# Cross-attention in pairs of batches: one projected chunk for two tails, and TensorE stages that take two or three chunks each

## The reference

```python
# B = 16 batches, 64 queries, H = 16 heads of HD = 32; context y: 1601 rows of 256 a batch
y_dca, y_main = y[:, -16:, :], y[:, :-16, :]           # 16 and 1585 rows
k_dca, v_dca  = _ln(head part of y_dca @ Wkv_dca), other part
q = _ln(x @ Wq + bq)                                   # per head, over 32
k = _ln(y_main @ Wk + bk); v = y_main @ Wv + bv        # per head
ctx = softmax(q k^T * SCALE) v + softmax(q k_dca^T * SCALE) v_dca
out = ctx @ Wo + bo
```

## Time and profile before

| | |
|---|---|
| median of 3 runs | 1699.8 us (1699.2 to 1699.86) |
| the profiled execution | 1697.8 us, its span 1695.9 us |
| PE busy | 1623.3 us (96% of the span) |
| PEld, DVE, ACT, POOL busy | 79%, 48%, 44%, 28% |
| mean granted clock | 0.983 |
| first scores to the end of cross-attention | 95.69 to 1274.66 us |

### The profile page before, as it was taken

One profiled execution on the slowest core, in us unless ns is written; L12 is line 12 of the kernel. 1 busy time (PEld: TensorE's weight loads), 2 busy tenths in 40 slices (PEclk: granted clock), 3 DMA queues, 4 the chain that ended last, 5 costly groups with the idle time before them and its releaser, 6 DMA issues. The chain is left out here.

```text
span 1695.9 us, 42180 instructions
## 1 busy us (share of the span) xinstructions
PE 1623.3 (96%) x16354; PEld 1338.6 (79%) x16354; DVE 811.3 (48%) x1841; ACT 749.7 (44%) x1523; POOL 472.1 (28%) x508
## 2 busy tenths in 40 slices
PE   5699999999999999999999999999995998899999
PEld 3378888888888888888888888888874666799998
DVE  6644444445444454544444444454543555433323
ACT  2255555555555555555555555555551333311111
POOL 2233332323333232333323232332324000022012
PEclk9899999999999999999999999999997999799999
DMA  6110000000000100000000000000001000111111
GB/s 220 50 56 15 27 28 27 15 27 27 15 27 28 27 15 27 27 15 27 28 27 15 27 27 15 27 28 27 3 2 56 1 0 1 57 56 38 33 41 49
DMA packets 33736, 53.50 MB, mean 32 GB/s; under 512 B 6963, under 2 KB 13494, under 8 KB 33590
## 3 DMA queue, kind: packets, MB, share of 16 engines
q1 hardware_dynamic: 33156, 51.20, 9.7%
q10 hardware_dynamic: 434, 0.08, 0.0%
HBM read 48.64 MB, written 2.62 MB: 30 GB/s over the span
## 5 line engine op out<-in xcount | busy, mean ns | idle before, releaser
L941 POOL TENSOR_TENSOR y_lo<-y_sb,y_hi 128x256 fp32r<-128x256 f32 (+1 forms) x206 | 146.7, 712 | 686.2 <-ACT y_hi L851 686.2
L883 ACT ACTIVATE probs<-psum 128x1024 f32<-128x1024 f32 x208 | 213.5, 1027 | 172.5 <-PE psum L1104 172.2
L991 DVE TENSOR_REDUCE kss<-ksq 128x16 f32<-128x512 f32 x208 | 142.7, 686 | 241.4 <-POOL ksq L948 241.4
L870 ACT COPY v_sb<-psum 128x512 f32<-128x512 f32 x192 | 112.7, 587 | 313.3 <-PE psum L96 313.2
L948 POOL TENSOR_TENSOR ksq<-kc 128x512 f32<-128x512 f32 x208 | 216.4, 1041 | 92.0 <-DVE kc L985 89.3
L1104 PE MATMUL psum<-qbd,k 64*128 64x128 f32 x3328 | 241.7, 285 | 0.0
L985 DVE TENSOR_TENSOR kc<-psum,bk_sb 128x512 f32<-128x512 f32 x208 | 143.7, 691 | 199.7 <-PE psum L96 199.7
L1120 PEld LDWEIGHTS psum<-v_sb,probs 128*64 128x64 f32 x6144 | 194.7, 138 | 33.4 <-issue 31.9
L1120 PE MATMUL psum<-v_sb,probs 128*64 128x33 f32 x6144 | 216.1, 224 | 1.1 <-ACT probs L883 1.1
L1104 PEld LDWEIGHTS psum<-qbd,k 64*128 64x128 f32 x3328 | 201.9, 187 | 8.9 <-issue 0.2
L96 PE MATMUL psum<-wk_hi,y_hi 128*128 128x512 f32 x416 | 187.2, 450 | 8.8 <-issue 8.7
(11 more groups left out here) (221 smaller groups left out, 2279.9 us busy)
## 6 DMA issues: line engine op xcount, KB each, us to landing
y_sb<-in_y SPq DMA_DIRECT2D x32, 512.0 KB, 3.5
y_sb<-in_y SPq DMA_DIRECT2D x16, 561.0 KB, 3.7
expert_raw<-in_wg SPq DMA_DIRECT2D x5, 768.0 KB, 4.7
expert_raw<-in_wu SPq DMA_DIRECT2D x5, 768.0 KB, 4.6
expert_raw<-in_wd SPq DMA_DIRECT2D x5, 768.0 KB, 4.5
out_dram<-x_sb SPq DMA_DIRECT2D x8, 256.0 KB, 2.0
x_sb<-in_x SPq DMA_DIRECT2D x1, 1536.0 KB, 9.6
wq<-in_wq SPq DMA_DIRECT2D x4, 256.0 KB, 4.4
```

What stands on the lines that cost most here:

```text
L870: nc.scalar.copy(g.v[:, c % VBUFS, :, 0:HD], bank).then_inc(s["ve"], 1)
L883: nc.scalar.activation(probs[:, buf(c), :], psum[:, S_BANK:S_BANK + 2, :].rearrange("p a n -> p (a n)"), ACT.Exp, scale=SCALE).then_inc(s[ ...
L941: nc.gpsimd.tensor_tensor(g.y_lo[:, buf(c), :, 0:w], y[:, :, c * P:c * P + w], g.y_hi[:, buf(c), :, 0:w].bitcast(F32), ALU.subtract).then_ ...
L991: nc.vector.tensor_reduce(ss[:, buf(c)], head_view(sq[:, buf(c)]), AX_X, ALU.add).then_inc(s["krd"], 1)
```

## The change

Batches are taken two at a time. A pair has UNITS = 26 chunks to score and weigh (13 a batch), but only PROJ = 25 to project and turn: the host puts the two 49-row tails into one 128-row array `y_tail` (rows 0 to 48 and 64 to 112), which is projected, squared, normalised and turned once. From it `k_evac` fills two key buffers (k32 2 and 3) and `v_evac` two halves of v_last, by two instructions each. The units of a pair form 12 groups, of 2, 2, 2, 2, 2, 3 chunks in each batch. For a group PE runs the projections of the group after the next, interleaved with the turns of the next group, then all `weighted` of this group, then all `scores` of the next. The scores alternate between two pairs of banks (3, 4 and 5, 6). That leaves one bank for the output: the tail's second half goes into V_BANK, and the turned result into TR_BANK. v has six buffers, o_evac is two copies, the DVE, ACT and POOL loops take a pair per iteration, with a hint for the back edge. DVE's new order has `k_norm` of a chunk behind `k_bias` of the next of its group. The queries of the next batch are copied at the start of the group of three, and `first` projects four chunks and scores two.

The core of the diff (functions of the new text that replace those of the old; renaming of `done` to `projected` and `unit`, and the guarded parts, left out):

```diff
-VBUFS = 4
+VBUFS = 6
+TAIL_ROWS, DCA_ROWS = (0, 64), (DCA_ROW, 0)
+TAIL, PROJ, UNITS = LAST, 2 * CH - 1, 2 * CH
+GROUP = [[u + CH * half for u in ((2 * n, 2 * n + 1) if n < 5 else (10, 11, 12))] for half in range(2) for n in range(6)]
+GR = len(GROUP)
...
-    K_BANK, V_BANK, TR_BANK, S_BANK, O_BANK, CT_BANK = 0, 1, 2, 3, 5, 7
+    K_BANK, V_BANK, TR_BANK, S_BANK, O_BANK = 0, 1, 2, 3, 7
...
-                    with eng.Fori(0, B - 1) as b:
-                        steps(b, CH, guarded)
-                steps(B - 1, 0, guarded)
+                    with nc.Fori(0, B // 2 - 1, engines=[eng.engine], hint_back_edge=True) as i:
+                        steps(i, GR, guarded)
+                steps(B // 2 - 1, 0, guarded)
...
+                def k_evac(i, n):
+                    i, n = at(i, n, PROJ)
+                    act.wait_ge(s["tr"], projected(i, n))
+                    bank = psum[:, TR_BANK, :].rearrange("p (g t) -> p g t", g=GROUPS)
+                    if tail(n):
+                        for half, first in enumerate(TAIL_ROWS):
+                            act.wait_ge(s["sc"], unit(i, same_tail((TAIL, UNITS - 1)[half])))
+                            last = nc.scalar.activation(k32[:, 2 + half, :, first:first + LM], bank[:, :, first:first + LM],
+                                                        ACT.Identity, scale=g.cols[:, 2:3], bias=g.cols[:, 3:4])
...
+                def o_evac(b, i, u):
+                    act.wait_ge(s["pv"], unit(i, u))
+                    act.wait_ge(s["on"], b + 1)
+                    nc.scalar.copy(o_sb[:, 1], psum[:, V_BANK, 0:PAIRS * VW1].rearrange("p (q n) -> p q n", n=VW1))
+                    nc.scalar.copy(o_sb[:, 0], psum[:, O_BANK, 0:PAIRS * VW1].rearrange("p (q n) -> p q n", n=VW1))\
+                        .then_inc(s["oe"], 1)
...
+                def steps(i, room, guarded):                     # ACT
+                    for group in range(GR):
+                        for j, u in enumerate(units(group, room)):
+                            exps(i, u, j)
+                        if group in (1, 7):
+                            ctx_evac(i * 2 + group // 6)
+                        project, turned, high = (projections(group + n, room) for n in (2, 1, 3))
+                        for j in range(3):
+                            if j < len(project):
+                                v_evac(i, project[j])
+                            if j < len(turned):
+                                k_evac(i, turned[j])
+                            if j < len(high):
+                                y_high(i, high[j])
+                            if j < len(project):
+                                seed(i, project[j])
+                        if group in (5, 11):
+                            o_evac(i * 2 + group // 6, i, GROUP[group][-1])
...
+                def chunks(i, ns):                               # DVE
+                    for j, n in enumerate(ns):
+                        k_bias(i, n)
+                        if j:
+                            k_norm(i, ns[j - 1])
+                        k_reduce(i, n)
+                    if ns:
+                        k_norm(i, ns[-1])
...
+                def scores(i, u, j, guarded):                    # PE
+                    i, u = at(i, u, UNITS)
+                    b = i * 2 + u // CH
+                    pe.wait_ge(s["ke"], projected(i, proj_of(u)))
+                    pe.wait_ge(s["ex"], unit(i, u - 1 if column(u) == 0 else u - 3 if column(u) == 1 else u - 2))
...
+                    bank = S_BANK + 2 * (j % 2)
...
                 def first(guarded):
                     keys(0, 0)
                     values(0, 0)
                     keys(0, 1)
                     values(0, 1)
-                    turn(0, 0)
                     keys(0, 2)
                     values(0, 2)
+                    turn(0, 0)
+                    keys(0, 3)
+                    values(0, 3)
                     turn(0, 1)
-                    scores(0, 0, guarded)
-
-                def steps(b, room, guarded):
-                    for c in range(CH):
-                        if ahead(c, 3, room):
-                            keys(b, c + 3)
-                            values(b, c + 3)
-                        if ahead(c, 2, room):
-                            turn(b, c + 2)
-                        if c == 2:
-                            turn_ctx(b)
-                        weighted(b, c)
-                        if ahead(c, 1, room):
-                            scores(b, c + 1, guarded)
+                    for j, u in enumerate(GROUP[0]):
+                        scores(0, u, j, guarded)
+
+                def steps(i, room, guarded):
+                    latest = PROJ - 1
+                    for group in range(GR):
+                        project, turned = projections(group + 2, room), projections(group + 1, room)
+                        if group in (1, 7):
+                            pe.wait_ge(s["ke"], projected(i, turned[0] - 1))
+                            turn_ctx(i * 2 + group // 6)
+                        for j in range(3):
+                            if j < len(project):
+                                keys(i, project[j])
+                                if j == 0 and group in (0, 6):
+                                    pe.wait_ge(s["oe"], i * 2 + (group // 6 + 1))
+                                values(i, project[j])
+                                latest = project[j]
+                            if j < len(turned):
+                                if j == 0 and group in (1, 7):
+                                    pe.wait_ge(s["ce"], i * 2 + (group // 6 + 2))
+                                turn(i, turned[j])
+                        for u in units(group, room):
+                            weighted(i, u, latest)
+                        for j, u in enumerate(units(group + 1, room)):
+                            scores(i, u, j, guarded)
```

More of the change, by code:

```diff
@@ L853, in k_evac @@
[L853 to L859, removed]
-                                         ACT.Identity, scale=g.cols[:, 2:3], bias=g.cols[:, 3:4]).then_inc(s["ke"], 1)
@@ new lines, in v_evac @@
+                def v_evac(i, n):
+                    i, n = at(i, n, PROJ)
+                    bank = psum[:, V_BANK, :].rearrange("p (h n) -> p h n", h=H)
+                    act.wait_ge(s["vp"], projected(i, n))
+                    if tail(n):
+                        for half in range(2):
+                            rows = slice(half * 64, half * 64 + 64)
+                            act.wait_ge(s["pv"], unit(i, same_tail((TAIL, UNITS - 1)[half])))
+                            last = nc.scalar.copy(g.v_last[rows, half, 0, :, 0:HD], bank[rows])
+                    else:
+                        act.wait_ge(s["pv"], unit(i, v_user(n)))
+                        last = nc.scalar.copy(g.v[:, (n - n // CH) % VBUFS, :, 0:HD], bank)
+                    last.then_inc(s["ve"], 1)
@@ L993, in k_norm @@
[L993 to L1001 removed]
+                    dve.sem_inc(s[stage], PROJ)
@@ L1047, in steps @@
+                def steps(i, room, guarded):
+                    for group in range(1, GR + 1 if room else GR):
+                        if group in (5, 11) and (group == 5 or room):
+                            queries(i * 2 + (1 if group == 5 else 2), i, TAIL if group == 5 else UNITS - 1, guarded)
+                        if group in (6, 12):
+                            dve.wait_ge(s["oe"], i * 2 + (group // 6 + 1))
                             nc.vector.reciprocal(rinv[:], o_sb[:, :, :, HD]).then_inc(s["rc"], 1)
+                        chunks(i, projections(group + 2, room))
+                        if group in (1, 2):
+                            second_keys(i, group - 1)
@@ L1084, in scores, with keys, values, turn @@
-                def scores(b, c, guarded):
-                    b, c = at(b, c)
-                    pe.wait_ge(s["ke"], done(b, c))
-                    pe.wait_ge(s["ex"], done(b, c - 1))
-                    if c == 0:
+                def keys(i, n):
+                    project(i, n, K_BANK, g.wk_hi, g.wk_lo, "kb", "kp")
+                def values(i, n):
+                    project(i, n, V_BANK, g.wv_hi, g.wv_lo, "ve", "vp")
+                def turn(i, n):
+                    i, n = at(i, n, PROJ)
+                    pe.wait_ge(s["km"], projected(i, n))
+                    pe.wait_ge(s["ke"], projected(i, n - 1))
+                    transposes(pe, psum[:, TR_BANK, :], kn[:, buf(n), :], g.ident[:]).then_inc(s["tr"], 1)
```

444 lines of the change are left out of this document (231 added, 213 removed).

## The result

The changed kernel takes 1621.88 us (median of 4 runs, 1621.35 to 1622.73) against 1699.57 beside it: 77.7 us less, ratio 0.9545, 95% interval 0.9533 to 0.9557. The forecast was 1634 (66 less), the range 1620 to 1662. The profiled execution took 1622.73, its span is 1620.9: 75.0 less than the span before, since the two profiled executions lie on the near sides of their medians.

The account below looks back on a forecast made before the run. PE was taken as the bound, busy 1172.88 of cross-attention's 1178.97 us. Removing 83.9 us and adding 17.8 gave 66.1 less than 1699.8, stated as 1634 us; own range 1625 to 1645, whole range 1620 to 1662.

Parts of the forecast that it names:

- (1): Shared tails: 200 projections and turns left of 208 on PE, 8 x (2.80 + 0.44) = 25.9 us less.
- (2): Seams between tilings on PE, paid per group instead of per chunk: 112 fewer at 0.46 us, 51.5 us less.
- (3): PE's stall for k_norm at a batch's end, removed by moving the queries' copy: 15 x 0.43 = 6.5 us less.
- (4): Group of three: the third scores wait for the first's exponentials, 16 x 0.45 = 7.2 us added.
- (5): Group of three in a pair's first batch: a turn directly behind another waits for k_evac, 8 x 1.2 = 9.6 us added.
- (6): V_BANK carries the tail's second output, so next values wait for o_evac: nothing added.
- (7): turn_ctx at a group's head costs its 0.2 us as before, POOL's normalising being done 9 us ahead.
- (8): Entry and end: 2 us of waits added at the entry, 1 us back at the end, net 1 us added.
- A: Seams are partly pipe latency that a second chunk pays again, so half that saving is lost: 1660 us; chance 0.12.
- B: Doubled loop bodies are fetched again at 7 back edges, making ACT late: 1634 to 1672 us, middle 1653; chance 0.15.
- C: ACT's k_evac comes late behind the first seed, PE waits 0.95 us in each of 96 groups: 1725 us; chance 0.05.
- D: The added waits of third scores and adjacent turns hide: 17 us less, 1617 us; chance 0.08.

Follow-up runs that it names:

- experiment 4: Changed kernel with the shared tail projected twice into the same bank, keys and values: 1643.66 us, ratio 0.9679 to the kernel before.
- experiment 3: Changed kernel with TensorE's weighted and scores by chunk again in 7 of a pair's 12 groups, none near a group of three: 1654.36 us.
- experiment 5: Kernel before, with VectorE's copy of the next queries moved behind k_norm and ahead of k_bias: 1692.57 us, ratio 0.9964 to the kernel before.
- experiment 7: Changed kernel with, before a group of three, the order weighted, two scores, weighted, third scores: 1619.61 us.
- experiment 6: Changed kernel with the three turns spread between keys and values, and k_evac ahead of v_evac on ScalarE there: 1612.0 us.
- experiment 1: Changed kernel with weighted and scores taken alternately within each group on TensorE: 1644.14 us, ratio 0.9689 to the kernel before.
- experiment 8: Changed kernel without the back-edge hint on the loops of ScalarE, VectorE and GpSimd: 1627.34 us.
- experiment 2: Changed kernel with TensorE's order by chunk again throughout, all other engines by group: 1711.99 us, ratio 1.0083 to the kernel before.
- the better version: Changed kernel with three edits together: turns spread, third scores apart, first two groups one list in VectorE's entry: 1607.1 us, ratio 0.9456 to the kernel before.

## Why the prediction was right, and where it was short

- **What bounds the kernel: right.** Twelve redundant matmuls a pair cost 21.8 us (experiment 4), 2.72 for each of the 8 pairs where 2.80 was taken.
- **(1) Shared tails, 25.9 us: right**: 21.8 by the same run, and 3.5 for the turns (8 x 0.44), which were not run by themselves, so 25.3.
- **(2) Seams, 112 x 0.46 = 51.5 us: the mechanism right, the size short.** This is the term that was mis-sized. It is 112 x 0.58 = 65, by the group's period and by experiment 3. The step at fault is the spacing. I divided a stage's starts evenly and took what was left over as the seam; but a stage starts slowly, and that slow start, paid only behind a change, went into the body. The second 16 records of `scores` add 1.98 - 1.09 = 0.89 us, not the 0.95 of the first; the second chunk's projections and turn take 617.67 - 614.49 = 3.18, against 2.80 + 0.44 in the sum and 606.56 - 603.13 = 3.43 as the first pays them. The upper bound for `scores` (0.12 more) was on the wrong side: doubling gained beyond the seam.
- **(3) The stall at a batch's end, 6.5 us: right**, 6.0 by experiment 5, and so was its cause.
- **(4) Third scores, 16 x 0.45: right**, 0.48 in the trace, and 0.42 by experiment 7 (2.3 us in 16, and 0.28 for the two changes more). **(5) Third turn, 8 x 1.2 = 9.6: right**, 1.17 in the trace and 9.9 us in experiment 6.
- **(6), (7), the rest hidden: right.** The group of two has no idle time before any PE row, and from 200 to 1150 us PE has no waits but those of (4) and (5). The layout was good to 0.3 us on ACT (the second `k_evac` ends at 7.54, not 7.8) and 0.5 on DVE (the second `k_norm` at 10.23, not 9.7); the slack covered both.
- **(8) The entry: the waits right, the clock left out.** First keys to the first group's first keys grew from 13.9 to 20.8 us; less a projection of 2.80 and a `scores` of 0.95 that is 3.1 lost, for 2 forecast. Of the 3.1, 1.5 is the stretch at half clock; what is left, 1.6, is less than the 2 of waits. At the end of cross-attention 0.2 came back in place of 1: three waits of 2.8 us together (0.59 for a turn, 1.12 each for exponentials) became one of 1.3, and the clock took 1.3 of what that gave. Both are by the trace of one execution; experiments 1 and 8 show that the clock does not fall in each.
- **The sum with the measured sizes:** 25.3 + 65 + 6.0 - 7.7 - 9.9 - 3.1 + 0.2 = 75.8 us. The entry and the end are from the traces, and the two profiled executions are 75.1 apart; the medians are 77.7 apart, and what the 2 us more are stays open.
- **Rivals.** A fell (experiments 1 and 3). B is a real mechanism on another engine, where 0.5 us of a back edge reaches PE and not 5.5, and the hint keeps it off. C was not there; experiment 2 shows that an order of ACT's list can make the kernel slower than before, by another wait than C's. D's 17 us of waits were all there, and are what the better version takes back.

The forecast missed the gain by 11.6 us (9.0 by the profiled executions). Item 2 alone is 13.5 the one way, and all the others together some 4 the other. The time fell below the forecast's own range of 1625 to 1645 and inside the whole range by 2 us. That it is inside is luck in part: the low end had been put there for D, whose waits did not hide, and the time came there by the price of the seams.

## What to carry to other kernels

Where the bound engine pays for each change of mode, price it by the difference of two periods (one item a round, two items a round), not by what is left when a round's mean spacings are added up: the slow start of each stage belongs to the change. When work is grouped, look for the place where the group is one larger than the rest; both added waits stood there, each for one buffer used twice in a row, and both went by reordering. And reorder the lists of all engines together. Where a busy engine is made to wait anew, at an entry or an end, look at the granted clock behind the wait too: here that cost 1.5 us behind a wait of 2.1, and 1.3 behind one of 1.3.

## What the runs showed that I had not expected

- The price of a change of tiling reaches into the records behind it: of the 0.58 us, 0.20 is in the stage of scores, whose first 16 records take 1.09 to the next stage and the second 16 only 0.89.
- A trace can name the wrong releaser: [1.01 <-DVE kn L1102] was ACT's copy, which ended 0.15 before, as experiment 6 shows.
- A loop of two batches without the hint makes DVE stand 3.7 us at each back edge, where loops of one batch brought no instruction packet at all, and the hint takes 64 packets in 950 us down to 5.
- Behind the waits at the entry and at the end the clock was halved for some 3.4 us, 2.8 us lost together, in a kernel whose clock I had taken to have nothing to give. Experiments 1 and 8 have one of the same waits each without it.
